# A graph network of two layers with windowed LSTMs on one core: statistics, hat passes, aggregates, norm passes and W2's passes placed elsewhere

## The reference, cut to what matters

```
h  = relu(layernorm(x))
h  = relu(adj @ (h @ Wg0 + bg0));  h = relu(adj @ (h @ Wg1 + bg1))
for p in 1, 2, 3, 4:       # windows of p tokens, one LSTM for each p
    last = the LSTM's last hidden state of every window of p tokens of h
    h[:, last token of each window] = last
x1 = x + h
A_hat = (adj + I) scaled on both sides by deg ** -0.5
z  = (A_hat @ relu(layernorm(x1))) @ W1.T + b1
z2 = relu(batchnorm(z)) @ W2.T + b2      # statistics over all batches and tokens
out = x1 + batchnorm(z2)
```

## Time and profile before

| | us |
|---|---|
| median of 3 runs | 526.07 |
| lowest and highest | 526.02, 527.83 |
| the profiled execution | 526.77 |
| its span in the profile | 524.9 |
| busy: TensorE, VectorE, ScalarE, GpSimd | 503.4, 413.5, 346.1, 198.2 |

### The profile page before, as it was taken

One profiled execution on the slowest core, in us unless ns is written; L12 is line 12 of the kernel. 1 busy time (PEld: TensorE's weight loads), 2 busy tenths in 40 slices (PEclk: granted clock), 3 DMA queues, 4 the chain that ended last, 5 costly groups with the idle time before them and its releaser, 6 DMA issues.

```text
span 524.9 us, 8041 instructions
## 1 busy us (share of the span) xinstructions
PE 503.4 (96%) x2720; PEld 429.3 (82%) x2720; DVE 413.5 (79%) x952; ACT 346.1 (66%) x672; POOL 198.2 (38%) x307
## 2 busy tenths in 40 slices
PE   6999997999999999999999999999999999999995
PEld 5788876989987789899887899999878998875574
DVE  3688788978868888786689887875898887976876
ACT  3646866756778577575686775767867676448744
POOL 6403035131401854343006750520553423337940
PEclk9999999999999999999999999999999999999999
DMA  7403000000011112010210101010714000600008
GB/s 234 129 21 101 1 1 20 22 0 22 1 60 42 40 61 81 2 51 31 79 62 23 44 37 61 1 62 33 268 42 140 21 2 21 242 0 1 0 13 310
DMA packets 17598, 31.22 MB, mean 59 GB/s; under 512 B 1514, under 2 KB 6292, under 8 KB 17428
## 3 DMA queue, kind: packets, MB, share of 16 engines
q1 hardware_dynamic: 16564, 30.17, 17.3%
q10 hardware_dynamic: 992, 0.52, 0.4%
HBM read 19.16 MB, written 11.53 MB: 58 GB/s over the span
## 4 chain that ended last, share of the span: by engine, by line
PE 51%; issue 20%; DVE 10%; POOL 8%; ACT 6%; POOLq 3%; DVEq 1%; DMA 1%; ACTq 0%
PE gate_ps L1285 10%; PE gate_ps L1281 10%; PE gate_ps L1282 10%; PE pre_ps L1281 4%; PE pre_ps L1282 4%; PE pre_ps L1285 4%; POOL x_pre L448 3%; POOLq L446 2%; PE post_ps L1281 2%; PE post_ps L1282 2%; PE post_ps L1285 2%; ACT gate L765 2%; PE pre_ps L1349 1%; DVE cell L1088 1%; DVE x_back L1273 1%
## 5 line engine op out<-in xcount | busy, mean ns | idle before, releaser
L765 ACT ACTIVATE gate<-gate_ps,gate_bias 128x256 f32<-128x256 f32 (+2 forms) x312 | 163.7, 563 | 35.9 <-PE gate_ps L1285 34.6
L1285 PE MATMUL gate_ps<-by_class_lo,wih_hi 128*128 128x256 f32 (+2 forms) x264 | 84.5, 320 | 4.2 <-POOL by_class_lo L478 4.2
L1281 PE MATMUL gate_ps<-by_class_hi,wih_hi 128*128 128x256 f32 (+2 forms) x264 | 84.6, 321 | 1.1 <-DVE by_class_hi L1064 1.0
L1282 PE MATMUL gate_ps<-by_class_hi,wih_lo 128*128 128x256 f32 (+2 forms) x264 | 83.6, 317 | 0.0
L780 ACT ACTIVATE gate<-cell 128x512 f32<-128x512 f32 (+2 forms) x88 | 45.4, 515 | 44.2 <-DVE cell L1088 21.9
L478 POOL TENSOR_TENSOR by_class_lo<-h,by_class_hi 128x256 fp32r<-128x256 f32 (+1 forms) x40 | 34.5, 863 | 79.8 <-ACT by_class_hi L778 79.8
L1281 PE MATMUL gate_ps<-hstep_hi,whh_hi 128*128 128x256 f32 (+2 forms) x192 | 60.6, 316 | 0.8 <-DVE hstep_hi L1107 0.8
L1285 PE MATMUL gate_ps<-hstep_lo,whh_hi 128*128 128x256 f32 (+2 forms) x192 | 60.9, 317 | 0.0
L1282 PE MATMUL gate_ps<-hstep_hi,whh_lo 128*128 128x256 f32 (+2 forms) x192 | 60.0, 312 | 0.0
L1285 PEld LDWEIGHTS gate_ps<-by_class_lo,wih_hi 128*128 128x128 f32 x264 | 49.9, 189 | 8.4 <-POOL by_class_lo L478 4.9
L1281 PEld LDWEIGHTS gate_ps<-by_class_hi,wih_hi 128*128 128x128 f32 x264 | 49.9, 189 | 5.7 <-DVE by_class_hi L1064 1.6
(11 more groups left out here) (321 smaller groups left out, 1294.8 us busy)
## 6 DMA issues: line engine op xcount, KB each, us to landing
x_pre<-in_x SPq DMA_DIRECT2D x16, 256.0 KB, 2.9
x<-in_x SPq DMA_DIRECT2D x16, 256.0 KB, 2.7
z_spill<-z_ring SPq DMA_DIRECT2D x8, 512.0 KB, 2.9
z_back<-z_spill SPq DMA_DIRECT2D x8, 512.0 KB, 5.4
x_spill<-x SPq DMA_DIRECT2D x12, 256.0 KB, 2.0
x_back<-x_spill SPq DMA_DIRECT2D x1, 3072.0 KB, 11.4
out<-x_back SPq DMA_DIRECT2D x11, 256.0 KB, 2.9
x<-in_adj SPq DMA_DIRECT2D x1, 1024.0 KB, 7.3
```

The source lines that it names most:

```text
L765: nc.scalar.activation(gate[:, tile_of(g), gt, 0:size], gate_ps[k % GATE_BANKS][:, 0:size], ACT.Tanh if gt == G_GATE else ACT.Sigmoid, bia ...
L1281: nc.tensor.matmul(ps, w[0], m[0], start=start, stop=False)
L1282: nc.tensor.matmul(ps, w[1], m[0], start=False, stop=False)
L1285: return nc.tensor.matmul(ps, w[0], m[1], start=False, stop=stop)
```

## The change

- Round 0's statistics of batches 6 and 7 are due at turns 5 and 10 instead of 6 and 12 (`EARLY_STATS`). The hat pass between cell and state of turn 6 is dropped and one behind turn 17 added, which moves the passes from turn 6 to turn 17 by one place.
- In rounds 1 and 2 the aggregates of the first two batches go from turns 6 and 9 to 7 and 10, and their products hid0 and hid1 from 7, 10 and 8, 11 to 8, 11 and 9, 12. In round 3, where exceptions hold, batch 8's hid0 goes from turn 8 to 9. The norm of each fourth batch goes from turn 17 to 18.
- GpSimd's norm of the second layer is in two parts, `post_scale` and `post_passes`. Where the turn after also makes a low part (batches 2 and 3 of a round), the four passes wait in `left_over` until behind that low part.
- W2's stage: order 2, the first split batch, has its high and low parts in halves, each with its own count; z2 of orders 3 and 9 goes from VectorE to ScalarE and that of order 10 from ScalarE to VectorE; order 13 goes from GpSimd to ScalarE.

```diff
@@ -106,17 +106,17 @@
 
 WHOLE = (0,) + tuple(range(1, BATCHES - 2, 2))
 KEPT_Z2 = tuple(range(BATCHES - SUMS, BATCHES))
-DVE_Z2 = (3, 6, 9)
+DVE_Z2 = (6, 10)
 ACT_Z2 = tuple(k for k in range(BATCHES) if k not in KEPT_Z2 + DVE_Z2)
 POOL_Y = (3, 6, 9)
 DVE_Y = 1
 ACT_Y = tuple(k for k in range(BATCHES) if k not in POOL_Y + (DVE_Y,))
 SPLIT = tuple(k for k in range(BATCHES) if k not in WHOLE)
-POOL_WHOLE = (9, 13)
+POOL_WHOLE = (9,)
 ACT_WHOLE = tuple(k for k in WHOLE if k not in POOL_WHOLE)
 DVE_HALVES = ((2, 0), (2, 1))
 ACT_HALVES = ()
-POOL_BATCHES = (4, 6, 8, 10, 9, 12, 14, 15, 13)
+POOL_BATCHES = (4, 6, 8, 10, 9, 12, 14, 15)
 POOL_HALVES = tuple((k, half) for k in SPLIT for half in range(HALVES) if (k, half) not in DVE_HALVES + ACT_HALVES)
 
 
@@ -133,6 +133,18 @@
 def piece_number(k, at):
 
     return k + 2 if k > 0 or at.start > 0 else 1
+
+
+def parts_of(j):
+
+    if j == 0:
+        return [(slice(half, half + 1), slice(half * T, (half + 1) * T)) for half in range(HALVES)]
+    return [(slice(0, HALVES), slice(0, HALVES * T))]
+
+
+def parts_made(j):
+
+    return j + (HALVES - 1 if j > 0 else 0)
 
 
 def halves_to(halves, k):
@@ -149,12 +161,21 @@
 
 PRE_POS = {"stats": (-5, 4, 6, 12), "norm": (-2, 6, 10, 16),
            AGG0: (0, 8, 13, 18), LIN0: (1, 10, 15, 19), LIN1: (2, 11, 16, 20), AGG1: (4, 12, 17, 21)}
-POST_POS = {"turn": (0, 1, 2, 3), "agg": (6, 9, 14, 19), "hid0": (7, 10, 16, 20), "hid1": (8, 11, 17, 21),
-            "norm": (5, 7, 12, 17), "stats": (3, 5, 9, 15)}
+POST_POS = {"turn": (0, 1, 2, 3), "agg": (7, 10, 14, 19), "hid0": (8, 11, 16, 20), "hid1": (9, 12, 17, 21),
+            "norm": (5, 7, 12, 18), "stats": (3, 5, 9, 15)}
 CARRIED = BATCHES - 2 * PER_ROUND - 1
 LAST_POS = {"turn": {BATCHES - PER_ROUND - 1: 4}, "agg": {CARRIED: 4, CARRIED + 1: 7, CARRIED + 2: 10, CARRIED + 3: 14},
-            "hid0": {CARRIED: 6, CARRIED + 1: 8, CARRIED + 2: 11, CARRIED + 3: 16},
+            "hid0": {CARRIED: 6, CARRIED + 1: 9, CARRIED + 2: 11, CARRIED + 3: 16},
             "hid1": {CARRIED: 6, CARRIED + 1: 9, CARRIED + 2: 12, CARRIED + 3: 17}}
+
+EARLY_STATS = {EARLY + 2: 5, EARLY + 3: 10}
+
+
+def pre_slot(kind, n):
+
+    if kind == "stats" and n in EARLY_STATS:
+        return EARLY_STATS[n]
+    return len(ORDER) * (n // PER_ROUND - 1) + PRE_POS[kind][n % PER_ROUND]
 
 
 def post_slot(kind, n):
@@ -166,7 +187,7 @@
 
 IN_PROLOGUE = [(kind, EARLY + b) for kind, spots in PRE_POS.items() for b in range(PER_ROUND) if spots[b] < 0]
 PRE_AFTER = [[(kind, n) for kind, spots in PRE_POS.items() for n in range(EARLY, BATCHES)
-              if len(ORDER) * (n // PER_ROUND - 1) + spots[n % PER_ROUND] == slot] for slot in range(N_SLOTS)]
+              if pre_slot(kind, n) == slot] for slot in range(N_SLOTS)]
 LEFT = LATE - 1
 LAST_TURNED = LATE - PER_ROUND
 IN_NEXT_TURN = range(LAST_TURNED, LATE)
@@ -176,8 +197,8 @@
 
 
 DINV_DIAG, DINV_ROWS = 2, 5
-HAT_BETWEEN = (6, 7, 10, 11, 12, 13, 16, 17, 18, 19, 20, 21)
-HAT_BEHIND = (6, 7, 12, 13)
+HAT_BETWEEN = (7, 10, 11, 12, 13, 16, 17, 18, 19, 20, 21)
+HAT_BEHIND = (6, 7, 12, 13, 17)
 HAT_SLOTS = sorted(HAT_BETWEEN + HAT_BEHIND)
 DEG_ROWS, DEG_HI, DEG_LO, DEG_DIAG = range(4)
 SPLITS = (AGG0, LIN0, LIN1, AGG1, "turn", "agg")
@@ -340,6 +361,7 @@
         z_out = [sem(f"z_out{i}") for i in range(PER_ROUND)]
         turn_mm, x1_ready = sem("turn_mm"), sem("x1_ready")
         tail_rstd, tail_y = sem("tail_rstd"), sem("tail_y")
+        post_rstd = sem("post_rstd")
         post_stats, post_y, post_nhi, post_nlo = (sem(f"post_{n}") for n in ("stats", "y", "nhi", "nlo"))
         agg_mm, agg_hi, agg_lo = sem("agg_mm"), sem("agg_hi"), sem("agg_lo")
         hid_mm, z_ready, z_stats = sem("hid_mm"), sem("z_ready"), sem("z_stats")
@@ -452,6 +474,18 @@
             def norm_pre(n):
                 layer_norm(n, x_pre[:, n % 2, :], x_pre[:, n % 2, :], mv_pre[n % 2], ln_pre[n % 2], pre_stats, pre_y)
 
+            def post_scale(n):
+                norm_scale(n, mv_post[n % 2], ln_post[n % 2], post_stats).then_inc(post_rstd, 1)
+
+            def post_passes(n):
+
+                pool.wait_ge(post_rstd, n + 1)
+                ln = ln_post[n % 2]
+                for c in range(CHUNKS):
+                    last = nc.gpsimd.tensor_scalar(y_post[:, c * P:(c + 1) * P], x1[:, n % PER_ROUND, c * P:(c + 1) * P],
+                                                   ln[:, 2, c:c + 1], ln[:, 1, c:c + 1], ALU.add, ALU.mult)
+                last.then_inc(post_y, 1)
+
             def norm_post(n, y):
                 layer_norm(n, y, x1[:, n % PER_ROUND, :], mv_post[n % 2], ln_post[n % 2], post_stats, post_y)
 
@@ -477,6 +511,7 @@
                 states, (hi, lo) = class_of(chain, q, c)
                 nc.gpsimd.tensor_tensor(lo, states, f32(hi), ALU.subtract).then_inc(later_lo, 1)
 
+            left_over = []
             for slot in range(N_SLOTS):
                 r, chain, p, step, sub, nb = TURNS[slot]
                 if slot in POOL_LO:
@@ -489,6 +524,9 @@
                     nc.gpsimd.tensor_copy(h32[:, chain, 0::2, sub], cell[:, tile_of(slot), 0:T // 2]).then_inc(even_done, 1)
                 if p >= 3 and step + 1 < p:
                     later_class(r, chain, p, step + 1)
+                for n in left_over:
+                    post_passes(n)
+                left_over = []
 
                 for at in NORMS_AFTER[slot]:
                     for kind, n in PRE_AFTER[at]:
@@ -496,7 +534,11 @@
                             norm_pre(n)
                     for kind, n in POST_AFTER[at]:
                         if kind == "stats":
-                            norm_post(n, y_post)
+                            post_scale(n)
+                            if makes_parts(slot + 1):
+                                left_over.append(n)
+                            else:
+                                post_passes(n)
 
             for n in range(LATE, LATE + 2):
                 norm_scale(n, mv_post[n % 2], ln_post[n % 2], post_stats).then_inc(tail_rstd, 1)
@@ -854,8 +896,9 @@
                         act.wait_ge(t_pool, halves_to(POOL_HALVES, k))
                     if j >= 3:
                         act.wait_ge(out_mm, SPLIT[j - 3] + 1)
-                    nc.scalar.activation(hid[j % 3][0][:, :, :].rearrange("p a t -> p (a t)"), z_end(b), ACT.Relu)\
-                        .then_inc(hid_hi, 1)
+                    for half, at in parts_of(j):
+                        nc.scalar.activation(hid[j % 3][0][:, half, :].rearrange("p a t -> p (a t)"), z_end(b)[:, at],
+                                             ACT.Relu).then_inc(hid_hi, 1)
                 if k + 1 in ACT_WHOLE:
                     whole_batch(k + 1)
                 if k - 2 in ACT_Z2:
@@ -1149,7 +1192,7 @@
                                 hid_stats(n, int(kind[-1]))
                 hat_steps(slot)
                 if slot in HAT_BEHIND:
-                    hat_step(*divmod(HAT_SLOTS.index(slot) + 1, CHUNKS))
+                    hat_step(*divmod(HAT_SLOTS.index(slot) + (slot in HAT_BETWEEN), CHUNKS))
 
             def tail_y_of(n):
 
@@ -1248,9 +1291,10 @@
             for k, b in enumerate(END_ORDER):
                 if k in SPLIT:
                     j = SPLIT.index(k)
-                    dve.wait_ge(hid_hi, j + 1)
-                    hi, lo = (part[:, :, :].rearrange("p a t -> p (a t)") for part in hid[j % 3])
-                    low(lo, z_end(b), hi, relu=True).then_inc(hid_lo, 1)
+                    for i, (half, at) in enumerate(parts_of(j)):
+                        dve.wait_ge(hid_hi, parts_made(j) + i + 1)
+                        hi, lo = (part[:, half, :].rearrange("p a t -> p (a t)") for part in hid[j % 3])
+                        low(lo, z_end(b)[:, at], hi, relu=True).then_inc(hid_lo, 1)
                 if k >= 2:
                     z2_stat(k - 2)
             z2_stat(BATCHES - 2)
@@ -1533,8 +1577,9 @@
                                                 start=half == 0, stop=half == HALVES - 1)
                 else:
                     j = SPLIT.index(k)
-                    pe.wait_ge(hid_lo, j + 1)
                     for half in range(HALVES):
+                        if half < len(parts_of(j)):
+                            pe.wait_ge(hid_lo, parts_made(j) + half + 1)
                         last = product(ps, [part[:, half, :] for part in w2], [part[:, half, :] for part in hid[j % 3]],
                                        half == 0, half == HALVES - 1)
                 last.then_inc(out_mm, 1)
```

## The result

| | before | after |
|---|---|---|
| median of 7 runs each, taken together | 527.83 | 524.0 |
| lowest and highest | 526.02, 531.18 | 522.92, 525.28 |
| the profiled execution | 526.77 | 525.25 |
| its span | 524.9 | 523.4 |

The ratio is 0.9935, with a 95% interval of 0.9913 to 0.9958: of these 527.83 us that is 3.4 us [2.2, 4.6] faster, where 5.4 was forecast. The 524.0 us lie 0.4 above the range's end at 523.6, and 3.3 above the forecast, 1.8 of them because the kernel before itself took 527.83 here and not 526.07. Taken from 526.07, the 3.4 us would have given 522.7, inside the range: that the time lies outside it is this shift, that the gain is two thirds of the forecast is what has to be explained.

A forecast was written before the change was run, and what follows sets the result against it. TensorE, busy 503.4 of 524.9 us, was taken as the bound, so only its waits could be gained. Terms 1.9 + 0.8 + 0.3 + 1.4 + 1.0 = 5.4 us off 526.07 gave 520.7 us, range 518.1 to 523.6.

The forecast's parts named there:

- Round 0, turns 7 to 10: Earlier statistics of batch 6 remove two TensorE waits, of 1.01 and 2.38 us; gain 2.1 us, bounds 1.2 and 3.2.
- Turns 11 to 13: Round 0: batch 7's statistics and the hat's adds delay u_lo; 0.8 to 0.9 us given back, bounds 0 and 1.5.
- Turns 14 to 17: Round 0: the 0.85 us low-part wait goes, the recurrent low part is next; gain 0.7 us, bounds 0.2 and 1.3.
- Rounds 1 and 2: First aggregate's norm wait goes, 0.55 us with restart, less 0.15 charged at turn 10; gain 0.4 us per round.
- Round 3, turn 8: Batch 8's first product behind turn 9 removes 0.50 us of waiting for agg_lo; 0.3 us remains, bounds 0 and 0.65.
- Round 3, turns 17 to 21: Batch 11's norm passes go behind the low part, removing a 1.00 us wait; gain 1.4 us, bounds 0.7 and 1.8.
- Rival 3: Norm passes beside the recurrence of turns 18 and 19 hold VectorE; round 3's 1.4 us goes: 522.1 us, chance 0.08.
- W2's stage: Halves of order 2 and new shares of passes make low parts sooner; gain 1.0 us, bounds 0 and 1.4.
- Rival 4: W2's stage is bound by ScalarE throughout and gains nothing: 521.7 us, chance 0.05.
- (2): Waits return elsewhere: round 0 gains 0.8 us, turn 10 of rounds 1 and 2 loses 0.2 each: 523.0 us, chance 0.2.
- (5): Slower: rounds 1 and 2, turns 7 and 10, queues stand for the aggregate and gates run late: 529.1 us, chance 0.05.
- the one for W2: Sign in the changed profile: first W2 product some 0.9 us after order 1's last matmul, later waits under 0.5 us each.

The follow-up runs named there:

- x12: The changed kernel with GpSimd's low parts of chain 0's first later class in round 0 (p = 3 and 4) cut to 4 token columns; 521.74 us.
- x6: The changed kernel with turn 11's pair of hat adds behind all else of that turn instead of ahead of its state; 521.94 us.
- x7: The kernel before with only the first two aggregates of the later steps and their products one turn later; 524.64 us.
- x3: The changed kernel with GpSimd's second-layer norm in one piece and each fourth batch's norm behind turn 17 again; 523.51 us, ratio 0.9921.
- x4: The changed kernel with GpSimd's low parts of later classes in round 3's four-token windows cut to 4 of 128 columns; 521.56 us in one run.
- x9: The changed kernel with evacuation and statistics of each W2 product one place later in ScalarE's and VectorE's queues; 521.34 us.

## Why the prediction was right in sign and too large

**Round 0, turns 7 to 10: 2.1 forecast, about 1.8 measured.** By the excess of each matmul's start over the pitch of its kind, summed over these turns, TensorE lost 4.2 us before and 2.4 in after. The waits lost their cause as described. What the step missed is in the next row: it let `hstep_hi` be late by the hat pass alone, and 0.72 us come from GpSimd's low part beside the product (x12).

**Turns 11 to 13: 0.9 given back forecast, 1.05 measured** as idle time and restart, for `u_lo`, and by the sum the text named: x6 moves the hat's adds, and the wait is gone.

**Turns 14 to 17: 0.7 forecast, 0.5 measured.** The adds of the hat stand ahead of turn 14's cell, as the text said, and GpSimd's low part beside it as well. Together round 0 gained 1.22 where 1.9 was forecast.

**Rounds 1 and 2: 0.4 each forecast, 0.89 and 0.85 measured.** The mechanism was right (x7 has it alone), the size too small. Of the 0.89, 0.70 lie at turn 6, where the text had 0.55: the loss beyond the idle time of 0.42 is 0.28 us and not 0.13. Another 0.12 lie at turn 9. And the 0.15 us charged for the low part of turn 10 was not needed; GpSimd's low part ends at 190.17 in after and nothing waited there.

```profile
188.99 1.18 POOL L512 TENSOR_TENSOR by_class_lo<-h,by_class_hi 128x340 fp32r<-128x340 f32 x1
```

**Round 3, turn 8: 0.3 forecast, 0.28 measured** for turns 0 to 14. By the excess of the starts, turns 8 and 9 lost 0.81 us before and 0.59 in after, so the move gained 0.22. In x3, which has the move too, the stretch gives 0.24 back at its end; the split of the norm passes keeps it, which the text counted at nothing in this place. That 0.28 met the forecast of 0.3 is so in part luck: by the move alone (x3) it would be 0.04.

**Round 3, turns 17 to 21: 1.4 forecast, 0.02 measured. This is the step that failed.** The text said that the chain of turn 18 comes over 1 us sooner and left the operations in it at their old durations. It did come sooner (the add of turn 18 by 0.88 us, counted from turn 15's first gate), and by that it moved onto GpSimd's low parts: the adds of turns 17 and 18, 0.42 and 0.43 us, became 0.77 each, while turn 19's met one in both kernels (0.87, then 0.79); and TensorE waits for `hstep_hi` twice instead of for `by_class_lo` once. With those low parts nearly gone 1.18 us appear (x4). About 0.4 of these belong to turn 19's meeting, which the kernel before had too, so the two new ones account for some 0.8 of the 1.4. The other 0.6 are a second fault of the same term: the text named the norm's low part that would now stand ahead of turn 19's state, and its 1.4, more than the 1.15 us of the wait alone, left no room for it; it costs 0.60 us between the adds of turns 18 and 19. Rival 3 had this outcome and the lock behind it, at a chance of 0.08, though with the wrong partner: it named the norm passes, whose move cost 0.1 us. The row at 440.79 that it rested on was itself an add beside a low part, and the text put it beside "a GpSimd pass" and priced the norm's four. Read by its own line number it gives nearly the right price, 0.44 us for each meeting, and a place for each: the low part of every turn.

**W2's stage: 1.0 forecast, nothing measured.** Order 2 starts 1.16 us sooner (3.27 for 4.43) and order 4 no sooner (7.84 for 7.74), as the text said; order 6 is 0.47 sooner, forecast 0.45. Then order 8 is 0.71 us later: order 3's evacuation now stands ahead of ScalarE's high part of order 6 (the second of the two at 482.99), so that of order 8, at 487.63, starts 12.47 us behind the stage's first matmul and not 11.79, and VectorE's low part takes 1.68 us beside a GpSimd pass, not 1.23. These rows of after carry it:

```profile
482.99 1.25 ACT L876 ACTIVATE z_ring<-gate_ps,vec 128x512 f32<-128x512 f32 x2
...
487.63 1.06 ACT L900 ACTIVATE hid_hi<-z_back 128x1024 fp32r<-128x1024 f32 x1
...
488.72 1.68 DVE L931 SCALAR_TENSOR_TENSOR hid_lo<-z_back,hid_hi 128x1024 fp32r<-128x1024 f32 x1 [0.22 <-ACT hid_hi L900]
```

The text took 2.42 us of ScalarE's idle time ahead of order 10 as room for the added passes. That room lies behind order 8; what was moved to ScalarE from order 3 comes ahead of it, where it ran without a gap at 3.50 us a pair of orders (high parts at 480.63, 484.13, 487.63) beside TensorE's 3.2. Rival 4, ScalarE bound and no gain, was the case that came, at a chance of 0.05; x9 shows that what bound was the order in its queue: at the same load 1.66 us are there to be had. This term failed in its path too: it read room off one idle stretch without asking which order's pass stands ahead of it.

**The rivals.** (2), at 523.0, came nearest in time, and for round 0's sum it held in part, but not for turn 10 of rounds 1 and 2. (3) and (4) both came true together, while the text gave each alone. (5) did not happen: the aggregates of turns 7 and 10 hold nobody (x7). (3) and (4) together, 520.7 with 1.4 and 1.0 back, are 523.1, and with the 0.7 that round 0 missed 523.8; that rounds 1 and 2 gave 0.94 us more than forecast hid part of this, by no merit of the sum. The range's low end took 1.0 for the last term of round 0, whose bound the text had put at 1.3; it decides nothing here. Of the signs, the one for W2 did not come: its later waits are 1.06, 0.20 and 0.62 us and not under 0.5 each.

## What to carry to other kernels

Before a wait is priced as removed, take the operations that move into the new time window and look at what runs beside them there: a chain that comes sooner meets other work, and here each meeting of a product or add of VectorE with GpSimd's low part cost 0.34 to 0.72 us on the chain. Room on an engine counts only ahead of the point where it is needed; read the pitch of the engine stage by stage, and try the order of its queue before moving work to another engine. And two rivals that act in different stages are not alternatives: their prices add, and the range needs the case in which both come.

## What the runs showed of the hardware

A VectorE product or add of two tensors is stretched by a GpSimd operation on two tensors beside it: 0.42 to 0.77 us (256 columns), 0.51 to 1.23 us (340 columns, with 0.92 us of GpSimd), and 0.51 again when GpSimd's takes 0.25 us (x12). It goes the other way too: GpSimd's low part at 434.62 took 1.03 us beside a VectorE product that was logged from 434.65 to 435.06 at its usual 0.41, and 0.73 us elsewhere. This is as if the two take turns. VectorE's statistics of 128 columns took 0.26 to 0.30 us each, beside a low part or not. The Trainium skill (SBUF — State Buffer, section "SBUF: two separate sides") has the port pair as an exclusive lock held for a whole instruction; the rows with two-tensor operations on both sides agree.

How much a meeting costs depends on the GpSimd instruction: low parts (two tensors in) cost up to their own length, the norm's passes (one tensor in, about 0.5 us each) 0.11, 0.15 and 0.13 us for the operations at 432.79, 433.37 and 433.84. If each pass locked VectorE out for its whole length, as that sentence has it, these could be held for up to 0.5 us each; why they are so much milder was not tried.

A TensorE that waited lost more than the idle time shown: at turn 6 of round 1, 0.42 us idle and 0.28 us more up to the old pace, where the prediction worked with 0.13 to 0.15.
